# Self-attention messages as one 128-column product per position, and x's second layout in 32 pieces

## The reference

```python
def _L0_attn_ref(x):
    b, c, l = x.shape
    q = jnp.transpose(x, (2, 0, 1))                        # (l, b, c)
    scores = jnp.einsum('lnc,lmc->lnm', q, q) / c ** 0.5   # per position, 32 x 32
    prob = jax.nn.softmax(scores, axis=-1)
    msg = jnp.einsum('lnm,lmc->lnc', prob, q)
    return x + jnp.transpose(msg, (1, 2, 0))
...
x = _layernorm(x + _L0_attn_ref(x), axis=-1)
x = _layernorm(x + _L0_xattn_ref(x, ctx_4096, ctx_4096, ...), axis=-1)
x = _layernorm(x + _L0_ffn_ref(x, w_gate, w_up, w_down), axis=-1)
```

## Time and profile before

| | |
|---|---|
| three runs, us | 670.32 median, 669.27 to 671.2 |
| profiled execution, us | 670.21, span 668.4 |
| busy share of the span | TensorE 91%, VectorE 84%, GpSimd 72%, ScalarE 71% |
| mean granted TensorE clock | 0.967 of full |
| x loads, second layout included | 8 issues of 1024 KB, 13.7 us to landing (median) |

### The profile page before, as it was taken

How to read it: one execution, slowest core, us unless ns; L and a number is a source line. 1 busy time by engine, 2 the same in 40 slices (tenths; PEclk the granted TensorE clock), 3 DMA queues, 4 the chain that set the end, 5 groups by cost and what they waited for, 6 DMA issues and landing times. The chain is left out here.

```text
span 668.4 us, 13138 instructions
## 1 busy us (share of the span) xinstructions
PE 607.3 (91%) x4855; PEld 333.8 (50%) x4864; DVE 558.9 (84%) x801; ACT 474.1 (71%) x871; POOL 479.0 (72%) x634
## 2 busy tenths in 40 slices
PE   0638999899999999999999999999999979999993
PEld 0638988444545445445545445445454534444441
DVE  2757999799999999999899879898788369999992
ACT  3208665788989989888988879888888735443535
POOL 1431778769889998998888686786778544776673
PEclk9956999899999999999999999999999989999998
DMA  8993032000001011110101000000000003345645
GB/s 315 173 212 113 2 111 62 11 17 25 1 19 53 10 32 40 41 41 25 40 13 45 1 23 17 7 17 16 1 1 1 9 8 60 76 94 99 134 103 132
DMA packets 62463, 36.76 MB, mean 55 GB/s; under 512 B 44736, under 2 KB 52928, under 8 KB 62400
## 3 DMA queue, kind: packets, MB, share of 16 engines
q1 hardware_dynamic: 62400, 35.93, 22.8%
HBM read 21.82 MB, written 4.19 MB: 39 GB/s over the span
## 5 line engine op out<-in xcount | busy, mean ns | idle before, releaser
L1932 ACT ACTIVATE big<-banks 128x512 f32<-128x512 f32 x288 | 158.7, 601 | 22.3 <-PE banks L2912 9.1
L663 POOL TENSOR_TENSOR big<-big 128x512 f32<-128x512 f32 x128 | 132.3, 1062 | 21.2 <-DVE big L1187 21.1
L1164 DVE TENSOR_REDUCE big<-banks 128x1 f32<-128x512 f32 x128 | 83.0, 679 | 21.9 <-PE banks L2879 21.7
L1993 ACT ACTIVATE big<-banks,big 128x512 f32<-128x512 f32 x128 | 88.0, 694 | 18.0 <-DVE big L1164 16.8
L655 POOL TENSOR_TENSOR big<-big 128x512 f32<-128x512 f32 x64 | 82.2, 1290 | 10.1 <-ACT big L1998 9.9
L1170 DVE TENSOR_REDUCE big<-banks 128x16 f32<-128x1024 f32 x64 | 77.1, 1205 | 4.9 <-PE banks L2889 4.8
L1175 DVE TENSOR_TENSOR big<-banks,big 128x1024 f32<-128x1024 f32 x64 | 78.3, 1223 | 2.7 <-PE banks L2922 0.7
L2912 PEld LDWEIGHTS banks<-ident,big 128*128 128x128 f32 x512 | 56.6, 142 | 47.2 <-issue 22.4
L2922 PEld LDWEIGHTS banks<-ident,big 128*128 128x128 f32 x512 | 55.2, 141 | 46.6 <-issue 22.7
L2912 PE MATMUL banks<-ident,big 128*128 128x128 f32 x512 | 74.2, 281 | 2.6 <-ACT big L1993 1.5
L1998 ACT ACTIVATE big<-big 128x1024 f32<-128x1024 f32 x64 | 68.1, 1065 | 10.2 <-DVE big L1175 9.7
(11 more groups left out here) (108 smaller groups left out, 1118.6 us busy)
## 6 DMA issues: line engine op xcount, KB each, us to landing
big<-in_x_dram SPq DMA_DIRECT2D x8, 1024.0 KB, 13.7
big<-in_ctx_dram SPq DMA_DIRECT2D x16, 256.0 KB, 2.7
out_dram<-big SPq DMA_DIRECT2D x16, 256.0 KB, 2.3
big<-in_L_ffn_w_down_dram SPq DMA_DIRECT2D x4, 688.0 KB, 10.2
big<-in_L_ffn_w_gate_dram SPq DMA_DIRECT2D x10, 256.0 KB, 3.0
big<-in_L_ffn_w_up_dram SPq DMA_DIRECT2D x10, 256.0 KB, 2.9
big<-big SPq DMA_TRANSPOSE x48, 2.7
wg_area<-in_L_xattn_Wq_dram SPq DMA_DIRECT2D x2, 128.0 KB, 10.8
```

The costliest lines, as they stand in the source:

```text
L663: pool.tensor_tensor(e, e, r, ALU.mult).then_inc(s.p_ready, 1)
L1164: dve.tensor_reduce(kneg[:, par, i:i + 1], bank[par], X, ALU.max, negate=True).then_inc(s.k_max_ready, 1)
L1932: return act.activation(dst, src, ACT.Copy)
L1993: act.activation(EK[:, f % 2, par, i], bank[par], ACT.Exp, bias=kneg[:, par, i:i + 1], accum_out=ksum[:, f % 2, par, i:i + 1]).then_inc(s. ...
```

## The change

The messages of a position become one product: the moving operand has all 128 columns (batch m, quarter j), and positions go by turns to PSUM partitions 0 to 63 (even ones) and 64 to 127 (odd ones). A bank then holds 4 pairs of positions x 128 columns instead of 8 positions x 64. So `add_msg` has four instructions instead of one: for each parity of the position (the half of PSUM) and each parity of the batch (the half of `xt`), 64 partitions x 64 x 4 elements, with a step of two positions in `xt`.

`xq` is loaded in 32 pieces of 8 channels of one quarter, 128 KB each, the quarters by turns, with three semaphores; a piece waits until the third before it has landed, so at most three are on their way. The first message waits for all.

```diff
@@ constants and semaphores
+    CQ = 8
-        s.xq_loaded = sem("xq_loaded")
+        s.xq_loaded = [sem(f"xq_loaded_{turn}") for turn in range(3)]
@@ SyncE
-            def load_xq(j):
-                sp.dma_start(xq[B * j:B * j + B], x[:, :, LG * j:LG * j + LG]).then_inc(s.xq_loaded, 16)
+            def load_xq(n):
+                c, j = CQ * (n // 4), n % 4
+                if n >= 3:
+                    sp.wait_ge(s.xq_loaded[n % 3], 16 * (n // 3))
+                sp.dma_start(xq[B * j:B * j + B, c:c + CQ], x[:, c:c + CQ, LG * j:LG * j + LG]).then_inc(s.xq_loaded[n % 3], 16)
...
-            load_xq(0)
-            load_xq(1)
-            load_xq(2)
-            load_xq(3)
+            for n in range(4 * C // CQ):
+                load_xq(n)
@@ VectorE, add_msg(c, h)
-                m = bank[(2, 6)[c % 2] + h].rearrange("p (l q) -> p q l", l=CL // 2)
-                l0 = CL * c + CL // 2 * h
-                r = xt.rearrange("p t (j l) -> p (t j) l", j=4)[:, :, l0:l0 + CL // 2]
-                dve.scalar_tensor_tensor(out=r, in0=r, scalar=2.0, in1=m, op0=ALU.mult, op1=ALU.add
-                                         ).then_inc(s.msg_added, 1)
+                m = bank[(2, 6)[c % 2] + h].rearrange("p (l b q) -> p b q l", l=CL // 4, b=2)
+                xl = xt.rearrange("p t (j l) -> p (t j) l", j=4)
+                for odd in range(2):
+                    l0 = CL * c + CL // 2 * h + odd
+                    for par in range(2):
+                        r = xl[C * par:C * par + C, :, l0:l0 + CL // 2 - 1:2]
+                        last = dve.scalar_tensor_tensor(out=r, in0=r, scalar=2.0, in1=m[C * odd:C * odd + C, par],
+                                                        op0=ALU.mult, op1=ALU.add)
+                last.then_inc(s.msg_added, 1)
@@ TensorE, messages(c, h)
-                    pe.wait_ge(s.xq_loaded, 64)
+                    for turn in range(3):
+                        pe.wait_ge(s.xq_loaded[turn], 16 * len(range(turn, 4 * C // CQ, 3)))
...
                 for l in range(CL // 2):
-                    for par in range(2):
-                        p = pd[:, c % 2, CL // 2 * h + l, :, T * par:T * par + T].rearrange("p j t -> p t j")
-                        last = pe.matmul(o[C * par:C * par + C, C * l:C * l + C], xq[:, :, CL * c + CL // 2 * h + l], p,
-                                         start=True, stop=True)
+                    rows, at = slice(C * (l % 2), C * (l % 2) + C), CL // 2 * h + l
+                    last = pe.matmul(o[rows, P * (l // 2):P * (l // 2) + P], xq[:, :, CL * c + at],
+                                     pd[:, c % 2, at].rearrange("p j m -> p m j"), start=True, stop=True)
```

## The result

The changed kernel takes 676.85 us (median of 4 runs, 676.43 to 677.35), the kernel before in the same comparison 669.80 (4 runs, 668.69 to 671.20). The ratio is 1.0086, interval 1.0065 to 1.0107: slower by 0.9%, where 672.6 was forecast.

The account below looks back on a forecast made before the run. The prediction held TensorE and VectorE both full in the message stage, with VectorE deciding after the change; -6.0 (front) + 9.5 (adds) - 1.1 (give-back) = +2.4 us on 670.2 gave 672.6 us, range 664.5 to 679.

Parts of the forecast that it names:

- the case: Whole kernel: adds cost more than the front gains, +2.4 us to 672.6, own range 669 to 676; chance 0.55.
- rival 2: Loading of x's second layout: pieces too slow, rounds of 4.5 us, last landing at 70 us, 681 us in all; chance 0.13.
- The front: Score stage before the first message product: 6.0 us gained, bounds nothing to 13.6 us.
- group 4 at 43.7: Step of the hand-made score schedule: fourth score group ends at 43.7 us, leading to scores' end at 63.3 us.
- Pacing: Loading x's second layout: 32 pieces, at most three under way, 3.1 us a round, 33 us, last landing at 55 us.
- The products: Message products on TensorE: 39.4 us fall to 30 us; the 9 us saved worth nothing by itself, VectorE being full.
- Rival 3: Message products: array halves don't overlap, TensorE bounds the second stage, 57 us there, 677 to 679 us in all; chance 0.07.
- The adds: Message adds on VectorE: 0.73 us more for each of sixteen, thirteen of them counting before clip_aw(3), 9.5 us.
- The give-back: VectorE before clip_aw(3): small L1088 at 110.37 us no longer meets a GpSimd instruction, 1.1 us returned.
- A shift reaches the end unchanged: From the first query product (122.67 us) on: edited lines do nothing, TensorE nearly always busy, so its shift reaches the end.
- Rival 1: Score stage: front gains far more than the adds cost, up to 13.6 us, 665.0 us in all; chance 0.25.
- The signs laid down: Trace: first message product 61 to 65 us, last add 116 to 119, TensorE idle 10 us or more, adds 0.33 to 0.41.

Follow-up runs that it names:

- the run with neighbouring reads: Kernel with the 32 paced pieces alone, its score products reading 32 neighbouring elements instead of 32 at a step of 512: 662.67 us, ratio 0.9872.
- every run of the table: Follow-up kernels, each measured against the kernel before; times from 662.67 us (ratio 0.9872) to 683.50 us (1.0187).

## Why the prediction was right, and where it was wrong

The forecast had the sign and the case: the adds cost more than the front gains. The size was off. The sum was +2.4 us, the medians differ by 7.05 and the spans by 6.7, more than the 3 us by which its terms were held to be uncertain. The 676.85 us measured lie 0.85 beyond the 669 to 676 that the prediction gave this case; they are inside the whole range only because that ran to 679 for rival 2, which did not happen. And of the 9.3 us at the first query product 2.6 were gone at the end, for which the forecast had no reason. Both were luck. Its terms, one after the other:

**The front: 6.0 us forecast, 4.3 measured.** That scores and the other engines get in each other's way was right, and the run with neighbouring reads shows it. What failed is the hand-made schedule: "group 4 at 43.7". The subtraction that group 4 waits for ended at 42.2 us instead, behind a clip (L1094) that was itself stretched by group 3, so group 4 waited 2.42 us, a wait that I had not laid down. Here is that clip:

```profile
35.80 4.56 DVE L1094 TENSOR_SCALAR big<-big 128x512 fp8e4<-128x512 f32 x1
41.59 0.69 DVE L1136 TENSOR_TENSOR big<-banks,big 128x512 f32<-128x512 f32 x1
```

From there the scores ran 3.0 us behind my plan (49.87 for 46.9, 56.90 for 53.9), and 1.5 us of stall without a named cause came on top, where the plan had 0.6, so messages started at 67.71 and not at 63.3. Since VectorE sets the next stage, the loss was smaller there: its transpose is 4.3 us earlier. The named mechanism, stretched instructions, was applied to the three instructions that I had looked at and not to the weight work between them.

**Pacing.** 33 us for the 32 pieces were forecast; SyncE issued them in 30.66 us, at 2.8 us from issue to landing, and nothing waited for them. Rival 2 is excluded. That the pacing is needed was the silent part of this step, and that was wrong: the size alone does it.

**The products.** Thirty-two records take 3.90 us in the message stage (at 98.54 us), 0.12 us each, 31 us for all 256: the 30 us that I took. Rival 3 is excluded, and its bound of 57 us with it. (Its time was also summed wrongly: the slack of 1.4 us is VectorE's, TensorE had 0.8. With that and the front's 6.0 us its case is 670.2 - 6.0 + 17.6 - 0.8 = 681 us, not 677 to 679.) The saving of 9 us came to TensorE as idle time (13.7 us), as forecast.

**The adds: the mis-sized term.** "four of 256 cost 4 x 0.33 = 1.32 us, or 4 x 0.41 = 1.64 if nothing overlaps" - and I took the first. The second was nearly right: 4 x 0.43 = 1.73, or +1.13 against 0.60. Thirteen of them cost 14.7 us and not 9.5. The duration of one was foreseen (0.42); that neighbours on different halves of the partitions don't overlap was not. Full partitions by 256 elements do have the 0.33 us (0.34), so the error lies in carrying an overlap measured on instructions that all start at partition 0 to adds that change the half each time.

**The give-back: 1.1 forecast, 3.0 measured.** -4.3 + 14.7 = 10.4 us, but the clip ended only 7.4 us later (119.96 against 112.55). The small L1090 (L1088 before) took less time: the one named 0.18 us at 119.00, where its counterpart took 1.30, and the one at 109.08 took 0.74 where it had taken 2.20. All nine of them from the transpose of chunk 4 to the clip, before and then after (count | busy us, mean ns):

```profile
L1088 DVE TENSOR_SCALAR big<-big 128x32 int32<-128x32 int32 x2 | 3.5, 1750 | 0.1
L1088 DVE TENSOR_SCALAR big<-big 128x43 int32<-128x43 int32 x2 | 3.1, 1552 | 0.1
L1088 DVE TENSOR_SCALAR big<-big 128x16 int32<-128x16 int32 x5 | 1.8, 352 | 0.2
```

```profile
L1090 DVE TENSOR_SCALAR big<-big 128x43 int32<-128x43 int32 x2 | 2.8, 1388 | 0.1
L1090 DVE TENSOR_SCALAR big<-big 128x32 int32<-128x32 int32 x2 | 0.9, 464 | 0.1
L1090 DVE TENSOR_SCALAR big<-big 128x16 int32<-128x16 int32 x5 | 0.9, 175 | 0.2
```

That is 8.4 us against 4.6, 3.8 us less, which is more than the whole 3.0; the difference goes in small amounts to other instructions, most of them beside the new adds. The long ones end with a GpSimd instruction (before, the one from 102.62 ends at 104.82 us beside one from 102.24 to 104.78; after, the one from 109.08 ends at 109.82 beside one from 107.29 to 109.79). The forecast counted one such meeting; the looser order shortened several.

**From the clip to the end.** `x1_rsqrt(0)` kept the 7.4 us, as forecast for a chain on GpSimd. The last three adds fell into its slack, as forecast, which went from 3.5 to 0.6 us. To the first query product it became 9.3, which the forecast did not have. `norm_x1(0)`, which that product had waited for, came 7.7 us later (from 129.49 to 130.30 us). But TensorE was not ready at its end. It had stood idle for 5.30 us, until the maxima behind the last three adds were there, and then ran at half clock: the eight transposes took 2.27 us where such eight took 1.09, the K products 2.08 for 1.13. With the times of such work at full clock (1.09 and 1.13, and 0.79 for the eleven transposes between them in another place) it would have been done at about 129.7, an estimate. So the idle time and the clock make the other 1.6 us. Then 0.8 us went between the first and the last query product (384.2 us for 385.0), and 1.8 behind it (158.9 for 160.7). That last part is not the change's doing as far as the runs show: the kernel before has its clock down after an idle stretch of 3.52 us, and the changed kernel has the same idle stretch without that. Windows of the same work, before and after:

```profile
535.00:547.00 12.00, 8.48 (x40) 4.29 (x39) 7.20 (x11) 3.56 (x7) 4.53 (x6) 0.86 0.06 11
```

```profile
543.50:555.50 12.00, 8.48 (x48) 4.39 (x48) 7.28 (x12) 4.07 (x8) 4.56 (x6) 1.00 0.06 11
```

Over all profiled kernels the time from the last query product to the end lies between 158.0 and 161.5 us. "A shift reaches the end unchanged" is true to 2 or 3 us, no better: in every run of the table, and for the change itself, the time moved by 0.8 to 2.9 us less upwards, or more downwards, than the query product did. All these shifts are taken from one execution of the kernel before, so it is open whether that one had its query product early. Of the 5.8 us that the pieces alone gain, the traces therefore show only some 3.

Sum by measured terms: -4.3 + 14.7 - 3.0 + 1.9 - 0.8 - 1.8 = +6.7. The errors in the forecast's own terms (+1.7, +5.2, -1.9) make 5.0 of the difference between +2.4 and +7.4 at the clip. Rival 1 stood on the front gaining 13.6 us; the earliest first message product of any kernel that computes the scores comes at 65.22 us, 3.7 early.

**The signs laid down.** TensorE was idle for more than 10 us in the message stage (13.7), and VectorE never waited for it there. But the first message product came at 67.71 us and not at 61 to 65, one gap without a cause was left (1.52 us), the adds were 0.43 us apart and not 0.33 to 0.41, and the last one ended at 125.1 us and not at 116 to 119.

The pieces by themselves are the better kernel, 665.0 us, or 665.9 without the pacing: 0.8% faster than the kernel before in both and some 1.6% faster than the changed one.

## What to carry to other kernels

A change that relieves an idle or equally full engine by putting instructions on the full one loses by the price of those instructions: count them, and price them in the very shape, partitions included, since a short instruction that lies on another half of the partitions than its neighbour doesn't overlap it. Unexplained idle time of TensorE beside a deep data queue can be removed by splitting the load into small transfers, at little cost, as long as TensorE doesn't go through its instructions much faster than here. But before counting that idle time as gain, lay down the whole list of the engines that work in its shadow.

## What the runs showed of the hardware beyond that

- TensorE's operand reads with a step of 512 fp32 elements (2 KB) take twice as long as neighbouring ones, 3.9 against 1.93 us per 128 records, and stretch what VectorE and ScalarE do beside them: a 0.69 us subtraction to 3.4 us (50.45 us in the changed kernel).
- VectorE: fp32 adds on the two halves by turns start 0.43 us apart (64 x 256) or 0.67 (64 x 512), those on all partitions 0.34 (128 x 256), 0.2 (128 x 128) or 0.60 (128 x 512). One instruction of 256 elements lasts 0.42 us on 64 and on 128 partitions.
- With the load in issues of 1 MB TensorE's unexplained stalls in the front are 14.0 us, with 512 KB 13.9, with 128 KB at most 1.5, paced or not. Where the score products read neighbouring elements and take half the time, they are 11.8 us with 128 KB as well.
- 32 issues of 128 KB took SyncE 20.3 us unpaced, 0.64 us each, and the data kept moving at about 205 GB/s; 8 issues of 512 KB took 17.7 us.
